# Spreading the gate/up weight generation over the layer norm and the QKV product of a sandwich transformer layer

## What is computed

```python
h = x + layernorm(attention(layernorm(x)))       # 16 heads of 128, causal, w_qkv and w_out dense
gate_w = spline_reconstruct(gate_cp, 8192, 2048) # 130156 control points -> 16.8 M weights
up_w   = spline_reconstruct(up_cp, 8192, 2048)
down_w = spline_reconstruct(down_cp, 2048, 8192)
y = (silu(z @ gate_w.T) * (z @ up_w.T)) @ down_w.T   # z = layernorm(h)
out = h + layernorm(y)
```

## Time and profile before

| | us |
|---|---|
| runs before, median of 2 (4326.60 and 4335.28) | 4330.94 |
| the profiled execution | 4332.67 |
| its span, first to last instruction, slowest core | 4331.1 |
| spans of the 8 cores | 4299.0 to 4331.1 |
| gate/up generation | 26 to 668 (and a start of 26) |
| layer norm and transposes | 680 to 796 |
| QKV product | 808 to 1365 |
| attention and all behind it | 1379 to 4331 |

### The profile page before, as it was taken

How to read it: one execution, slowest core, us unless ns; L and a number is a source line. 1 busy time by engine, 2 the same in 40 slices (tenths; PEclk the granted TensorE clock), 3 DMA queues, 4 the chain that set the end, 5 groups by cost and what they waited for, 6 DMA issues and landing times.

```text
span 4331.1 us, 41498 instructions; the slowest of 8 cores (4299.0 to 4331.1 us)
## 1 busy us (share of the span) xinstructions
PE 2991.0 (69%) x12618; PEld 1164.5 (27%) x12832; DVE 1440.7 (33%) x1876; ACT 924.6 (21%) x1519; POOL 531.7 (12%) x968
## 2 busy tenths in 40 slices
PE   3444442699997666666913333599998829999895
PEld 0111111344443111111400000244443314444332
DVE  6666667422222443442074555301100040101002
ACT  3444443000001333333113333100000020000001
POOL 6555550000000000000002222000000000000000
PEclk9999999999998777777955555699999969999997
DMA  8898884554442000002459998444434434444344
GB/s 172 193 205 188 206 198 148 88 76 78 77 77 73 30 20 30 30 20 39 68 163 153 173 173 165 158 154 156 149 114 126 131 131 175 150 152 146 108 137 144
DMA packets 346408, 538.51 MB, mean 124 GB/s; under 512 B 44208, under 2 KB 259248, under 8 KB 331568
## 3 DMA queue, kind: packets, MB, share of 16 engines
q1 hardware_dynamic: 226768, 397.55, 26.9%
q0 software_dynamic: 119424, 138.29, 22.4%
HBM read 405.40 MB, written 134.22 MB: 125 GB/s over the span
## 4 chain that ended last, share of the span: by engine, by line
PE 50%; DMA 25%; DVE 15%; issue 4%; POOL 3%; ACT 2%; DVEq 0%; SPq 0%; ACTq 0%; another core or an unknown queue 0%; POOLq 0%
PE pq L687 12%; PE puE L1085 11%; PE pgE L1079 10%; DMA gi<-gct 8%; DMA di<-dct 8%; PE pdE L1128 6%; DMA wdsb<-wbuf_d 6%; PE prow L222 3%; DVE gwo L443 3%; PE pav L226 3%; PE po L901 3%; PE psc L822 3%; DVE rs L857 2%; POOL gi L160 2%; DVE colsb L236 2%
## 5 line engine op out<-in xcount | busy, mean ns | idle before, releaser
L1085 PE MATMUL puE<-x2f,wusb 128*128 128x512 bf16 x2048 | 778.7, 380 | 16.7 <-DMA wusb<-wbuf_u 12.5
L1079 PE MATMUL pgE<-x2f,wgsb 128*128 128x512 bf16 x1966 | 747.4, 380 | 0.0
L687 PE MATMUL pq<-x2T,wq 128*128 128x512 bf16 x2508 | 551.6, 380 | 15.6 <-DMA wq<-wqkvT 13.0
L422 PE MATMUL pguA<-Ug,atsb 16*128 16x512 bf16 x512 | 296.3, 580 | 357.5 <-DVE gwo L443 330.8
L1128 PE MATMUL pdE<-actsb,wdsb 128*128 128x512 bf16 x2006 | 459.0, 382 | 69.4 <-DMA wdsb<-wbuf_d 66.6
L551 PE MATMUL pdnA<-Ud,atsb 16*128 16x512 bf16 x256 | 147.9, 580 | 338.8 <-DVE Ud L519 296.8
L443 DVE CAST_PREDICATED gwo<-gm,pguA 128x512 bf16<-128x512 uint8 x512 | 353.8, 691 | 70.8 <-ACT gwo L438 18.2
L438 ACT CAST gwo<-pguB 128x512 bf16<-128x512 f32 x512 | 299.6, 585 | 341.0 <-PE pguB L422 245.5
L1100 DVE TENSOR_TENSOR actsb<-silsb,puE 128x512 bf16<-128x512 bf16 x128 | 88.0, 688 | 814.0 <-ACT silsb L1095 814.0
L687 PEld LDWEIGHTS pq<-x2T,wq 128*128 128x128 bf16 x2560 | 250.7, 98 | 316.4 <-issue 16.0
L422 PE MATMUL pguB<-Ug,atsb 16*128 16x512 bf16 x512 | 308.0, 603 | 0.0
(11 more groups left out here) (82 smaller groups left out, 2285.1 us busy)
## 6 DMA issues: line engine op xcount, KB each, us to landing
wgsb<-wbuf_g SPq DMA_DIRECT2D x128, 512.0 KB, 3.3
wusb<-wbuf_u SPq DMA_DIRECT2D x128, 512.0 KB, 4.2
wdsb<-wbuf_d SPq DMA_DIRECT2D x128, 512.0 KB, 3.8
gi<-gct POOLq DMA_DIRECT2D x512, 64.0 KB, 6.6
wbuf_g<-gwo SPq DMA_DIRECT2D x64, 512.0 KB, 12.2
wbuf_u<-gwo SPq DMA_DIRECT2D x64, 512.0 KB, 12.0
wbuf_d<-dwo SPq DMA_DIRECT2D x32, 1024.0 KB, 20.5
wq<-wqkvT POOLq DMA_DIRECT2D x24, 1024.0 KB, 10.4
```

The source lines that it names most:

```text
L422: t.matmul(pp[:, :], at_sb[u_:u_ + 16, :], U[b][u_:u_ + 16, cc:cc + 512], start=True, stop=True, tile_position=(u_, 0)))
L687: t.matmul(pq[bi][:, :], wq[(o // 2) % 2][:, h * 256 + (o % 2) * 128: h * 256 + (o % 2) * 128 + 128], x2T[:, h * S + g * 512:h * S + g * 5 ...
L1079: t.matmul(pg[bi][:, :], wg[o % 4][:, h * 128:h * 128 + 128], x2f[:, h * 512:h * 512 + 512], start=(h == 0), stop=(h == 15)))
L1085: t.matmul(pu[bi][:, :], wu[o % 4][:, h * 128:h * 128 + 128], x2f[:, h * 512:h * 512 + 512], start=(h == 0), stop=(h == 15)))
```

## The change

The gate/up generation loses its own stage. The generator is made inside phase B, with 2 banks for each of `pguA` and `pguB` and not 4 (the other 4 banks of PSUM are used by `ptr`, then `pq`), and it is advanced by 3 steps in each of the 16 layer norm tiles, between the layer norm and the transposes of the tile before, and by 12 steps in each output chunk of QKV: ahead of each of the first 6 matmuls of both groups for oc below 16, and ahead of each of the first 3 matmuls of the four groups from oc 16 on. The call of 24 steps after QKV stays; by then the generator has nothing left. The number of generated chunks, of instructions for each, and of SBUF buffers stays the same.

```diff
--- before.py
+++ after.py
@@ -592,21 +592,16 @@
         qscope = ctx.enter_context(contextlib.ExitStack())
         q_all = qscope.enter_context(
             nc.sbuf_tensor("qall", [128, H * TPC], BF16))
-        if "W" in PHASES:
-            with contextlib.ExitStack() as wsc:
-                pguA = [wsc.enter_context(
-                    nc.psum_tensor(f"pguA{i}", [128, 512], F32))
-                    for i in range(4)]
-                pguB = [wsc.enter_context(
-                    nc.psum_tensor(f"pguB{i}", [128, 512], F32))
-                    for i in range(4)]
-                gugen = make_gu_gen(wsc, pguA, pguB, depth=4)
-                for _ in range(NGCH * 9 + 20):
-                    next(gugen)
-            sch.barrier()
-
         if "B" in PHASES:
             with contextlib.ExitStack() as bc:
+                pguA = [bc.enter_context(
+                    nc.psum_tensor(f"pguA{i}", [128, 512], F32))
+                    for i in range(2)]
+                pguB = [bc.enter_context(
+                    nc.psum_tensor(f"pguB{i}", [128, 512], F32))
+                    for i in range(2)]
+                gugen = make_gu_gen(bc, pguA, pguB, depth=2) \
+                    if "W" in PHASES else None
 
                 x2T = bc.enter_context(nc.sbuf_tensor("x2T", [128, 16 * S], BF16))
                 xt = [bc.enter_context(nc.sbuf_tensor(f"xt{i}", [128, D], F32))
@@ -659,6 +654,9 @@
                         _emit_ln(sch, col, 8 * bufp, xt[bufp][:, :],
                                  lnsqs[bufp], out_bf=lnsqs[bufp])
                         nmks[ti] = sch.mark("V")
+                        if gugen is not None:
+                            for _ in range(3):
+                                next(gugen)
                         if ti >= 1:
                             b_transpose(ti - 1)
                     b_transpose(15)
@@ -680,9 +678,12 @@
                         tgs = [0, 2] if oc < 16 else [0, 1, 2, 3]
                         kind, hh = oc // 16, oc % 16
                         sch.wait("T", wtok[oc // 2])
+                        npump = 12 // len(tgs)
                         for tix, tg in enumerate(tgs):
                             sch.wait("T", evtix.get((oc - 1, tix)))
                             for hc in range(16):
+                                if gugen is not None and hc < npump:
+                                    next(gugen)
                                 sch.op("T", lambda t, h=hc, o=oc, g=tg, bi=tix:
                                        t.matmul(
                                            pq[bi][:, :],
```

## The result

The changed kernel takes 0.963 [0.961, 0.965] of the time before, measured beside it on the same chip: 4161 to 4174 us against 4318 to 4343. The profiled execution took 4166.07 us with a span of 4164.5 (cores 4146.2 to 4164.5); 4,160 was forecast. Executions in which the cores of a die ran some per cent longer at a lower clock are left out of the times (e9 and e11 had no others, and for them the spans of the other die's cores are given), but e1's 4123 and e8's 4384 and 4402 are kept, and the profiles of e2 and e8 are of cores that ran so.

What follows compares the result with a forecast made beforehand. The old generator stage was taken as DMA-bound, QKV as PE-bound. QKV starting at 256 plus 935 us (291 + 590 + 54) ends at 1,191 against 1,365, 174 less: 4332.7 - 174 = 4,159, rounded 4,160; range 4,070 to 4,300.

Steps and rivals of the forecast that it cites:

- Bounds of the stages: Generator stage bound by DMA (busy 0.87) with DVE close behind, QKV by PE; the change lays one over the other.
- The pair on PE: In QKV, a pguA/pguB pair costs PE 0.41 us, including two weight-shape changes of 0.09; ends 0.22 and 0.74.
- Rival 2: Each change of tiling drains the PE array, so a pair costs 0.74 us: kernel 4,220 us; chance 0.14.
- The depth wait: In QKV, pair i waits for the write of pair i-2, round trip 2.19 us; K/V groups 5.62 or 4.27 us.
- the 590 that I took for the DMA: QKV from oc 16 on, without the bare part: 590 us taken, as DMA's 557 stands close to PE's 580.
- The layer norm: Three tiles with steps take 42.5 us, including x load stalls of 5 and 6; first QKV matmul at 256 us.
- The highest share of any such stage is 0.87, so these need 291 and 557 us: In QKV, DMA work of 253 us below oc 16 and 485 above is stretched to 291 and 557 us.
- Rival 1: PE falls back to 1.2 GHz in the mixed stream: about 4,550 us, slower than before; chance 0.08.
- if only oc below 16 fell, it would be +30: A fall to 1.2 GHz in QKV's oc below 16 alone adds 30 us, inside the range.
- Rival 4: DMA and PE hinder each other more: late expansions, PE waiting for banks, x stalls of 8: 4,300 us; chance 0.15.
- Rival 3: Waits smaller than taken: x loads land in 5.6 us, DMA keeps up, 256 becomes 225, 935 becomes 884: 4,080; chance 0.18.
- Behind QKV: Everything from the attention on has the same instructions and is taken at its old time.

Runs made afterwards that it cites:

- e9: Changed kernel with three banks each for pguA and pguB, no layer norm steps, 8 steps per Q chunk, 14 per K/V chunk: 3936 to 3969 us on cores 0-3.
- e11: Changed kernel with the six steps of a Q group split, ahead of matmuls 0, 1, 2 and 8, 9, 10: 4100.6 to 4120.8 us on cores 4 to 7.
- e1: Changed kernel with steps spread: ahead of matmuls 0, 3, 6, 9, 12, 15 in Q groups, 0, 5, 10 in K/V groups: 4067 to 4074, 4123 us; 0.943.
- e8: Kernel before, with 2 banks instead of 4 for each of pguA and pguB in its own generation stage: 4338 to 4347, 4384, 4402 us; 1.005.
- e2: Changed kernel without steps in the layer norm; those 48 steps move to the end of the generation, inside QKV: 4113 to 4124 us; 0.951.
- e4: Changed kernel with three banks instead of two for each of pguA and pguB, and two instead of four for pq: 4038 us; 0.933.
- e3: Changed kernel with the next tile's x load issued ahead of the layer norm steps' stores on SP's queue: 4126 to 4144 us; 0.955.
- e5: Changed kernel without tap loads and expanding DMAs from chunk 2 on (generated weights wrong): 4163 to 4171 us; 0.963.

## Why the prediction was right, and where it was not

- **Bounds of the stages.** Right in what the sum needed: a stage with little PE work was laid over one bound by PE, and both together now take 1,202 us instead of 1,365. That DMA as such bounded the old stage is not shown: in e8 DVE's wait for gi nearly went, at much the same length of the stage, and nothing here tells what held the share at 0.87.
- **The pair on PE.** 0.41 forecast, 0.42 measured. Rival 2 is out: at a change of tiling 0.32 us pass in both directions. The Trainium skill, "TensorEngine Tiling (Array Packing)", Key Properties, says that a change of mode drains the engine; this trace shows no more than 0.10 us lost at each change (0.32 less 0.216).
- **The depth wait.** Right to 0.04 us: third pair at 2.19 (the terms as listed add up to 2.18), groups of 5.64, 5.58 and 4.31 against 5.62, 5.62 and 4.27. K, V and the bare part took 639 us; PE's terms alone gave 580 + 54 = 634. e4 shows that the wait was the cause. With the 590 that I took for the DMA, 644 had stood there.
- **The layer norm.** 42.5 forecast for three tiles behind tile 0 (the first term, 17.2, should be 16.9 by its own parts), 41.0 measured; stalls of 5 and 6, measured 5.5 and 4.1 in the tiles shown and 5.0 on the mean of the nine; first QKV matmul 256, measured 251. e3 shows the cause of the stalls.
- **The step that failed: "The highest share of any such stage is 0.87, so these need 291 and 557 us".** The work of the DMA engines was right: 253 us forecast for the Q part, 0.82 x 313 = 257 measured; 485 for K and V, 0.84 x 557 = 468 measured. The Trainium skill, "DMA: Bandwidth & Descriptors", Issuing engines are not separate DMA queues, says that DMAs run on the same 16 engines whichever engine started them; the trace agrees in that the busy times of the two stages' DMAs add. But 0.87 was what that stage had needed, not what the engines can give: e1 and e4 reached 0.96 and 1.00. And e5 shows that DMA was no limit in QKV of the changed kernel. Only PE's term, 250 us, was a bound of the Q part, and it assumed 2.4 GHz.
- **The term that was missing there: the clock.** The Q part took 312 us. Waits for DVE were 54, and PE was busy 257, against 204 in e11 (core 6) at a clock of 0.92: some 50 us by matmuls at 1.2 GHz. Rival 1 came true in this part, wholly in half of its groups. The prediction had priced it, "if only oc below 16 fell, it would be +30", and the sum held since a term that was too high for one reason (291 in place of 250) stood where another was missing (62). Two errors cancelled to 21 us: that the total came out within 7 us is luck in this part. From oc 16 on the clock stayed up, as argued, over waits of 0.8 us with 3.2 us of dense matmuls behind each.
- **Rivals 3 and 4.** Rival 4 is out: DVE waited 11 us for gi; PE waited for wq only at the start of QKV (13.8 us, against 11.3 before), although the landing took 15.7 us at the median, not 10.4. Rival 3 was half right: DMA did keep up in QKV (e5), but the x loads did not land in 5.6 us each (first QKV matmul 251, not its 225, which by stalls of 2.6 and 3.2 should have been 230), and the clock took from the Q part what DMA did not: 951 us, not 884.
- **Behind QKV.** Unchanged to 3 us, as taken.

The profiled execution is 7 us over the 4,159 of the sum: QKV's beginning gave -5, the Q part +21, K and V -5, and what lies behind -3, to a us of rounding.

## What to carry to other kernels

When a stage is spread through another, look up what its buffers' depth hid behind: here two banks cost some 15 us in the old place (e8) and some 125 against three in the new one (e4), since there the waits stood in the order of the engine that bounds. A DMA share read from a stage tells what the stage asked for, not what the engines can give; take some DMAs away to find out. And put the added steps where they cost the bounding engine of that stage least, in short runs with dense work between: here a burst of waiting matmuls cost those behind it the clock.

## What the runs showed of the hardware that was not expected

- The DMA engines reached a share of 1.00 over 252 us (e4), with loads, converting loads, on-chip expansions and stores mixed.
- In the Q part of the changed kernel, where behind the first wait for wq no gap was over 1.8 us, TensorE went to 1.2 GHz again and again, at 297.77 us after gaps of 0.47, 0.30 and 0.41, and came back within one group; the same pairs split into two runs of three raised the granted clock from 0.75 to 0.92 (e11, core 6), at gaps of up to 2.4 us.
- The granted clock stands at 1.00 in the generation stage of before, while its matmuls take 0.58 us: there the length of a matmul tells the clock, the column does not. In the layer norm of the changed kernel the column reads 0.60 to 1.00 on the eight cores, with PE busy for 49.2 to 50.1 us on each.
- The 1 MB converting load of wq took 10.4 us to land at the median in the kernel before, 15.7 in the changed kernel, 12.7 with half the DMA share (e5) and 18.8 in e1.
